# A mean pass over graph edges: the edge product as two products of 64 rows in two PSUM banks, and the sums in one bank

## What is computed

```
msg    = relu(concat(h[dst], edge_attr_16) @ W1 + b1)     # 64 + 16 -> 64, per edge
summed = segment_sum(msg, dst); count = segment_sum(1, dst)
aggr   = summed / max(count, 1)
x      = x + relu(aggr + h @ Wres + bres)
```

## Time and profile before

| | |
|---|---|
| runs | 6828.68 to 6829.21 us, median 6829.01 |
| profiled execution | 6818.34 us, span 6816.5 us |
| TensorE busy (PE) | 4422.8 us, 65% of the span |
| VectorE busy | 4366.3 us, 64% |
| ScalarE busy | 1118.9 us, 16% |
| GpSimd busy | 4726.5 us, 69% |
| TensorE's mean granted clock | 0.538 of full speed |

### The profile page before, as it was taken

One profiled execution on the slowest core, in us unless ns is written; L12 is line 12 of the kernel. 1 busy time (PEld: TensorE's weight loads), 2 busy tenths in 40 slices (PEclk: granted clock), 3 DMA queues, 4 the chain that ended last, 5 costly groups with the idle time before them and its releaser, 6 DMA issues. The chain is left out here.

```text
span 6816.5 us, 149747 instructions
## 1 busy us (share of the span) xinstructions
PE 4422.8 (65%) x36620; PEld 3475.0 (51%) x36620; DVE 4366.3 (64%) x15732; ACT 1118.9 (16%) x4722; POOL 4726.5 (69%) x5116
## 2 busy tenths in 40 slices
PE   7996666666666667666666666667666666666665
PEld 5775444444444446444444444446444444444444
DVE  5556666666666666666666666666666666666666
ACT  3222111111111112111111111112111111111111
POOL 1224777777777775777777777775777777777776
PEclk9995555555555555555555555555555555555555
DMA  4553333333333333333333333333333333333333
GB/s 128 159 159 96 95 95 95 96 95 95 95 96 95 96 95 98 95 95 95 95 95 95 95 95 95 95 96 97 95 95 95 95 95 96 95 95 95 96 96 80
DMA packets 687682, 675.79 MB, mean 99 GB/s; under 512 B 369234, under 2 KB 506388, under 8 KB 687636
## 3 DMA queue, kind: packets, MB, share of 16 engines
q0 software_dynamic: 161600, 320.52, 18.3%
q1 hardware_dynamic: 496944, 301.76, 16.3%
q10 hardware_dynamic: 29092, 52.97, 2.6%
HBM read 652.96 MB, written 21.67 MB: 99 GB/s over the span
## 5 line engine op out<-in xcount | busy, mean ns | idle before, releaser
L1621 POOL DMA_INDIRECT Gall<-KV,sdn x4848 | 4590.0, 947 | 1517.0 <-issue 1380.9
L754 DVE TENSOR_TENSOR kj<-Gall,pE 128x512 f32<-128x512 f32 x603 | 414.4, 687 | 1973.4 <-DMA Gall<-KV,sdn 1971.3
L963 PE MATMUL pG<-O,vals 128*66 128x42 f32 (+1 forms) x10736 | 1291.9, 308 | 0.7 <-ACTq L1242 0.7
L963 PEld LDWEIGHTS pG<-O,vals 128*66 128x66 f32 (+1 forms) x10736 | 1200.8, 223 | 47.4 <-ACT vals L1002 28.4
L948 PE MATMUL pY<-fw,Ob 128*42 128x6 bf16 (+1 forms) x4800 | 255.1, 176 | 1139.9 <-DVE cr L807 1139.9
L994 ACT ACTIVATE vals<-dd 128x16 f32<-128x16 f32 (+1 forms) x606 | 131.6, 217 | 4679.5 <-DVE dd L834 4671.0
L948 PEld LDWEIGHTS pY<-fw,Ob 128*42 128x42 bf16 x4800 | 220.4, 121 | 1192.9 <-issue 1192.9
L896 PE MATMUL pE<-bd,ea 128*128 128x256 f32 x1212 | 739.9, 714 | 13.6 <-PEq L1242 13.6
L955 PEld LDWEIGHTS pM<-Mb,OTs 42*128 42x128 bf16 x4800 | 176.3, 101 | 921.1 <-issue 921.1
L901 PE MATMUL pE<-bd,ea 128*128 128x256 f32 x1212 | 642.8, 634 | 0.0
L955 PE MATMUL pM<-Mb,OTs 42*128 42x6 bf16 (+1 forms) x4800 | 209.9, 163 | 514.2 <-DVE df L825 511.8
(11 more groups left out here) (223 smaller groups left out, 6539.9 us busy)
## 6 DMA issues: line engine op xcount, KB each, us to landing
db<-D SPq DMA_DIRECT2D x606, 256.0 KB
ea<-in_ea SPq DMA_DIRECT2D x606, 128.0 KB
Gall<-KV,sdn POOLq DMA_INDIRECT x4848
db<-D ACTq DMA_DIRECT2D x202, 256.0 KB, 3.5
qw<-QT SPq DMA_DIRECT2D x1818, 5.2 KB
dr<-in_dr SPq DMA_DIRECT2D x1212, 4.0 KB
ea<-in_ea SPq DMA_DIRECT2D x202, 64.0 KB, 3.3
sdn<-in_sdn SPq DMA_DIRECT2D x606, 12.0 KB
```

What stands on the lines that cost most here:

```text
L754: return e.tensor_tensor(kj[:, :, :], G[u][:, :, 0:64], pE[u][:, :].rearrange("p (j c) -> p j c", c=64), ALU.add)
L963: return e.matmul(out[0:AR, 0:W], vals[u][:, j, 0:AR], O[u][:, j, :], start=j == 0, stop=j == T - 1)
L1621: e.indirect_dma_start(G[u][:, j, :], None, kvtab, bass.IndirectOffsetOnAxis(ap=sdn[u][:, j:j + 1], axis=0)).then_inc(s_g[u], 16)
```

## The change

The banks are named in pairs, pair[u] = banks 2u and 2u+1; the names pE, pY, pQ and pS then point to the same six places as before. In the mean pass the edge product of slot u is two products: rows 0 to 64 of `ea` and bd16 give the groups 0 to 3 (256 columns) in the first bank of the pair, rows 64 to 128 the groups 4 to 7 in the second. The q products follow into the two banks, the relu reads 256 columns of each. With six banks used up so, the sums of all slots go to pG, and the first sum product of a block waits for the accumulation of the block before; both of its waits get a hold.

```diff
--- before.py
+++ after.py
@@ -151,10 +151,9 @@
     fb = [sb(f"fb{u}", [W, 66]) for u in range(3)]
     dd = sb("dd", [128, T, 2])
 
-    pE = [pb(f"pE{u}", [128, T * 64]) for u in range(3)]
-    pY = pb("pY", [128, 512])
-    pQ = pb("pQ", [128, 512])
-    pS = pb("pS", [128, 512])
+    pair = [pb(f"pair{u}", [128, 1024]) for u in range(3)]
+    pE = [pair[0][:, 0:512], pair[0][:, 512:1024], pair[1][:, 0:512]]
+    pY, pQ, pS = pair[1][:, 512:1024], pair[2][:, 0:512], pair[2][:, 512:1024]
     pG = pb("pG", [128, 512])
     pM = pb("pM", [128, 512])
     pAT = pS[0:16, 0:128]
@@ -690,7 +689,7 @@
         pos = {k: {o[2:]: n for n, o in enumerate(order[k])} for k in order}
         K = {k: len(order[k]) for k in order}
         NL = 6 if att else 1
-        sums = [pG, pG, pG] if att else [pG, pQ, pY]
+        sums = [pG, pG, pG] if att else [pG, pG, pG]
         columns = pIo if att else iof[:, 0:W]
 
         def val(k, o, s):
@@ -894,7 +893,10 @@
             ge16(e, s_e, 1, s)
             if att:
                 return e.matmul(pE[u][:, 0:256], ea[u][:, 0:128], bd32[:, l, :], start=True, stop=True)
-            return e.matmul(pE[u][:, :], ea[u][:, 0:128], bd16[:, :], start=True, stop=False)
+            for h in range(2):
+                p = e.matmul(pair[u][:, 512 * h:512 * h + 256], ea[u][64 * h:64 * h + 64, 0:128],
+                             bd16[64 * h:64 * h + 64, 256 * h:256 * h + 256], start=True, stop=False)
+            return p
 
         def p_e1(e, s):
             u = s.slot
@@ -917,9 +919,11 @@
                 hold(e)
                 ge16(e, s_l, NL, s)
                 hold(e)
-            out = pQ if att else pE[u]
-            return e.matmul(out[:, 64 * j:64 * j + 64], OTs[u][:, j, :], qw[u][:, :],
-                            start=att, stop=att or j == T - 1)
+            if att:
+                out = pQ[:, 64 * j:64 * j + 64]
+            else:
+                out = pair[u][:, 64 * j + 256 * (j // 4):64 * j + 256 * (j // 4) + 64]
+            return e.matmul(out, OTs[u][:, j, :], qw[u][:, :], start=att, stop=att or j % 4 == 3)
 
         def p_aT(e, s):
             u = s.slot
@@ -959,6 +963,9 @@
             u = s.slot
             if j == 0 and not att:
                 after(e, "A", "relu", s)
+                hold(e)
+                after(e, "V", "acc", s - 1)
+                hold(e)
             out = sums[u] if out is None else out
             return e.matmul(out[0:AR, 0:W], vals[u][:, j, 0:AR], O[u][:, j, :], start=j == 0, stop=j == T - 1)
 
@@ -999,7 +1006,9 @@
         def a_relu(e, s):
             u = s.slot
             after(e, "P", "q", s)
-            return e.activation(vals[u][:, :, 0:64], pE[u][:, :].rearrange("p (j c) -> p j c", c=64), ACT.Relu)
+            return e.activation(vals[u][:, :, 0:64].rearrange("p (h j) c -> p h j c", h=2),
+                                pair[u][:, :].rearrange("p (h b j c) -> p h b j c", h=2, b=2, c=64)[:, :, 0, :, :],
+                                ACT.Relu)
 
         dV, dP, dA = (sem(f"{name}_drain_{k}") for k in "VPA") if att else (None, None, None)
         nV = place(["fhi1", "fm1", "flo1", "cr1", "d1_2", "d_2", "flag0", "vals2", "facc3", "acc3",
```

## The result

The changed kernel takes 7085.91 us (median of 4 runs, 7074.16 to 7089.07), the kernel before 6828.85 (four executions; the 6829.01 of the table above is the median of the first three): a ratio of 1.0372, interval 1.0359 to 1.0384, or 257 us more. The forecast was 6858 and slower; the time lies outside its range and near the rival "the clock falls" (7048, chance 0.06). One of the 52 executions of the kernel before, here and beside the experiments, stands apart, with 7030.90 us at a mean granted clock of 0.507, where the other eight on its chip took 6816 to 6823 us at 0.536 to 0.539; it is left out of the ratios.

The account below looks back on a forecast made before the run. SyncE's issuing was taken to bound the mean pass at 2.236 us a step; the new step, 0.45 + 0.60 + 0.37 + 0.96 = 2.38 us, over 202 steps adds 29 us to 6829, giving 6858, range 6833 to 6876.

Parts of the forecast that it names:

- the clock falls: Rival: thinner TensorE work drops its clock to 1.2 GHz for the mean pass, 219 us more, 7048; chance 0.06.
- The pace: Mean pass of the kernel before: SyncE's issuing sets the step at 2.236 us, TensorE's chain lying just under it.
- The chain of 2.10 us: TensorE's mean-pass step from q to q before the change: 0.45 + 0.60 + 0.05 + 0.09 + 0.91 us.
- The price of the two waits: Before the sums: two held waits put the weight load 0.37 us behind the relu instead of 0.05.
- the accumulation's wait: Before a block's first sum product: the previous accumulation ends 0.5 us ahead of the load, so this wait is always met.
- the overlap of the halves: Edge product: 0.47 us side by side or 0.94 in turn; either way the sums start no earlier.
- SyncE giving way: Mean pass: SyncE stops pacing, with 0.14 us of air at the new 2.38 us step; slower pass, chance 0.77.
- the third rival: The rival "the clock falls"; its quoted step argued against a whole pass at half clock; chance 0.06.
- 0.63 + 0.60 + 0.37 + 1.72: Mean-pass step at half clock: relu start, relu, waits, sums to q; 3.32 us in all.
- The term that fell short most: In the half-clock step: the two waits between the relu's end and the sums' load, put at 0.37 us.
- the two terms taken from the pass's first step: In the half-clock step: relu start 0.63 us and sums to q 1.72 us, read from rows at half clock.
- worth nothing: Mean pass: work the change takes away from TensorE gains no time, as SyncE paces at 2.236 us.

Follow-up runs that it names:

- e7: Kernel before, with the edge attributes of blocks 3 and on issued from ScalarE's queue; 25 us less than the kernel before, ratio 0.9962.
- e10: Changed kernel, relu's wait on the weight load, 12 added full-width products in the pass's first step; -1 us against the kernel before, ratio 1.0001.
- e12: e7 again on the chip of e11: kernel before with edge attributes on ScalarE's queue; -32 us against the kernel before, ratio 0.9970.
- e1: Kernel before plus only the one bank for the sums and both held waits, edge product unsplit; +39 us against the kernel before, ratio 1.0039.
- e3: Changed kernel, but both edge products take all 128 rows (added rows are zeros); +31 us against the kernel before, ratio 1.0036.
- e8: Changed kernel plus 22 added full-width products in each of the pass's first three steps; +55 us against the kernel before, ratio 1.0081.
- e9: Kernel before with one bank for the sums, accumulation's held wait first, relu's wait on the weight load; -5 us against the kernel before, ratio 0.9997.
- e5: Changed kernel, but both edge products use rows 0 to 64, so one after the other; +428 us against the kernel before, ratio 1.0628.
- e6: Changed kernel with a single edge product of 128 rows by 256 columns, no second one; +237 us against the kernel before, ratio 1.0348.
- e2: Changed kernel with the two waits turned round, the relu's riding on the weight load; +254 us against the kernel before, ratio 1.0278.
- e11: e10 with the edge attributes issued from ScalarE's queue; -26 us against the kernel before, ratio 0.9972.
- e4: Changed kernel with its pair of half products issued twice per step; +32 us against the kernel before, ratio 1.0037.

## Why the prediction was wrong

**Right, by the runs.** The pace: SyncE, not TensorE (e7; e10 with the short product at full clock changes nothing). The chain of 2.10 us (e7 and e12 run at 2.11). The price of the two waits at full clock: 0.37 us behind the relu forecast, 0.36 measured; step 2.38 forecast, 2.37 measured (e1, e3, e8). That the accumulation's wait itself is always met (e9). That the overlap of the halves decides nothing at full clock (e8 with the halves side by side takes 2.374 us, e3 with two full products one after the other 2.381); at half clock it is worth 0.85 us a step (e5), which the prediction, with "it has no price here", had at nothing. SyncE giving way (the spread of its two issues in the changed kernel).

**Wrong: the chance of the clock, and two of its reasons.** The step that failed is this one of the third rival: "in a cold step the engine would be busy again for most of the time, and a rise follows". In the changed kernel TensorE is busy 708 of 714 us and no rise follows. By that reason the clock stood in the forecast's sum at nothing. I took the busy column for what decides the clock. e3 and e5 send the same columns through TensorE one after the other: on 128 rows the clock rose, on 64 it did not, with TensorE busy 400.00 of 400 us; e6, with half of the columns on all rows, did not rise either. The other reason was the question itself: I asked whether the clock would fall to half. The earlier trace rows already had the pass begin at 0.50, so the change had only to stop a rise, and in both executions of e8 no fall came. Half of the work of the longest product was enough to keep the clock from rising at the pass's entry, in all four executions, and I gave that 0.06.

**The size of that rival** was 7048, measured 7086. Its sum had 0.63 + 0.60 + 0.37 + 1.72 = 3.32 us; measured 0.67 + 0.60 + 0.45 + 1.78 = 3.50. The term that fell short most is the third, and by another cause than it names: not the waits but the edge product holds the load (e2, e5). It starts 0.57 us behind q (301.08 to 301.65), where before it was 0.25 at full clock, and the sums begin 1.15 us behind it. e6 has the same waits and a product that streams as long (1.20 us), on full rows:

```profile
302.90 0.58 PEld L925 LDWEIGHTS pair<-qw,OTs 128*128 128x128 bf16 x8
...
303.40 0.53 PEld L896 LDWEIGHTS pair<-bd,ea 128*128 128x128 f32 x2
...
303.68 0.60 ACT L1008 ACTIVATE vals<-pair 128x512 f32<-128x512 f32 x1 [2.81 <-PE pair L925]
304.63 1.83 PEld L969 LDWEIGHTS pG<-O,vals 128*65 128x65 f32 x16 [0.70 <-issue]
```

Its product's load (303.40) starts before the q loads end (302.90 + 0.58 = 303.48), and the sums' load comes 0.35 us behind the relu's end (303.68 + 0.60 = 304.28), close to the 0.37 of the forecast's term. In the changed kernel the product's load (301.64, second line) waits until the q loads have ended (300.98 + 0.58 = 301.56, first line):

```profile
300.98 0.58 PEld L926 LDWEIGHTS pair<-qw,OTs 128*128 128x128 bf16 x8
...
301.64 0.51 PEld L897 LDWEIGHTS pair<-bd,ea 64*128 64x128 f32 x4
```

The steps differ by 0.09 us (3.497 and 3.407), 18 of the 38 us by which the rival was short. The Trainium skill, page TensorEngine Tiling (Array Packing), Key Properties, says that a change of tiling mode drains the engine. The traces agree as far as the start goes: in e11, at full clock, the product starts 0.34 us behind q (302.30 to 302.64) instead of 0.25, and at half clock the changed kernel's starts 0.57 behind it, where e6's starts 0.44 behind (303.01 to 303.45). I had put that drain at nothing for the sum, which is right at full clock, where the relu covers it, and wrong at half. The rest of the shortfall lies in the two terms taken from the pass's first step, 0.63 and 1.72 us; e6 too has 0.67 and 1.79.

In the forecast's own terms, then: removed by the change, nothing; added, 27 us of waits, as forecast, where the clock is up; and where it isn't, 253 us of clock, in which the waits vanish. What the change takes away from TensorE, "worth nothing" by the prediction, is what cost the clock.

## What to carry to other kernels

Before thinning TensorE's work, look at the granted clock where the stage begins: a stage that enters at half clock can stay there, as here for 714 us with TensorE busy 708 of them, and a thinner product may be what decides it. Shorten an engine only once the profile shows that its chain sets the step; here a queue with no listed wait and a constant distance between its issues did, and one issue moved off it was worth 25 us where halving the largest product was worth nothing. Of several waits ahead of an instruction, put the one that is always met first, in a semaphore instruction of its own, and let the late one ride on that instruction: e1's step of 2.376 us became 2.239 in e9.

## What the runs showed of the hardware

- One and the same loop ran for hundreds of us at 1.00 behind added work at its entry (e8) and at 0.50 without it, 2.374 against 3.497 us a step (e8 and the changed kernel; two and four executions): what TensorE did at the entry decided.
- In passes entered at 0.50, an edge product on 64 rows, side by side (the changed kernel) or one after the other (e5, TensorE busy 400.00 of 400 us), left the clock there, and so did one of 128 rows and half of the columns (e6, 398.74); with 128 rows and all columns it rose and was at 1.00 with 385.90 busy (e3), and with the pair of half products twice it rose too (e4, 399.97). Once up it held with 379 of 455 (e8).
- Two products on different row halves began within 0.05 us of each other (the changed kernel). The first product of 64 rows behind those of 128 started about 0.09 us later than one of 128 rows does at full clock (e11, 0.34 against 0.25), and 0.13 later at half clock (0.57 against 0.44 in e6).
- A weight load of TensorE came 0.12 us behind its releaser with the wait in a semaphore instruction of its own, 0.36 with two such waits and a register addition between them (e1), 0.05 with the wait on the load itself (e11).
